# One graph and mixing block on one core: the mixing weights' product moved to the start, the value product ahead of the context sums, and 21 visits moved into the first graph layer

## The reference, cut to what matters

```python
xn = layernorm(x)
# mixing branch
q = softmax(xn @ Wq.T, axis=-1) * 512 ** -0.5
k = softmax(xn @ Wk.T, axis=-2)            # over the rows
v = xn @ Wv.T
context = k.T @ v                          # 512 x 512
y = q @ context + xn
mix = y @ W1.T @ W2.T + y
# graph branch, two layers
h = xn @ gW1.T + gb1
agg = segment_sum(h[src], dst)             # = A @ h, A counts the edges
z = relu(agg)                              # and again with gW2, gb2
x = x + graph + mix
# then a routed expert layer on layernorm(x), in the last third of the span
```

## Time and profile before

| | us |
|---|---|
| median of 3 runs | 469.31 (467.96 to 470.11) |
| the profiled execution's own time | 468.61 |
| span of its profile | 466.8 |
| TensorE busy | 451.0 of the span (97%) |
| VectorE busy | 320.9 (69%) |
| ScalarE / GpSimd busy | 150.6 / 63.1 |
| granted TensorE clock, mean | 1.00 in the profile's rows |

### The profile page before, as it was taken

How to read it: one execution, slowest core, us unless ns; L and a number is a source line. 1 busy time by engine, 2 the same in 40 slices (tenths; PEclk the granted TensorE clock), 3 DMA queues, 4 the chain that set the end, 5 groups by cost and what they waited for, 6 DMA issues and landing times.

```text
span 466.8 us, 6816 instructions
## 1 busy us (share of the span) xinstructions
PE 451.0 (97%) x2424; PEld 360.6 (77%) x2424; DVE 320.9 (69%) x1104; ACT 150.6 (32%) x272; POOL 63.1 (14%) x90
## 2 busy tenths in 40 slices
PE   7999999999999999999999999999999998878995
PEld 3788778888888888888779999877777776655783
DVE  6995699899998988897752110444645666777972
ACT  4686453322323332332222110222133114551110
POOL 4088200000000000000004000002300000006642
PEclk9999999999999999999999999999999999999999
DMA  8902002911000000001200000002744449305891
GB/s 219 287 1 91 1 0 91 219 50 65 2 1 1 1 1 1 1 2 20 108 0 4 1 1 1 1 0 53 277 139 134 134 142 380 131 1 190 289 356 71
DMA packets 20846, 40.46 MB, mean 87 GB/s; under 512 B 2953, under 2 KB 3283, under 8 KB 20805
## 3 DMA queue, kind: packets, MB, share of 16 engines
q1 hardware_dynamic: 18549, 32.55, 22.4%
q0 software_dynamic: 2256, 7.39, 4.5%
HBM read 30.10 MB, written 10.31 MB: 87 GB/s over the span
## 4 chain that ended last, share of the span: by engine, by line
PE 86%; DVE 8%; ACT 2%; issue 1%; DMA 1%; SPq 0%; POOLq 0%; DVEq 0%
PE ps L736 46%; PE ps L1031 9%; PE ps L957 9%; PE ps L848 5%; PE ps L723 5%; PE ps L1167 2%; ACT scrap_a L1424 1%; PE ps L1048 1%; PE ps L1137 1%; DMA X<-in_x 1%; PE ps L880 1%; PE ps L770 1%; PE ps L984 1%; PE ps L1008 1%; PE ps L1078 1%
## 5 line engine op out<-in xcount | busy, mean ns | idle before, releaser
L1713 DVE TENSOR_SCALAR RING_D<-places,PLACES 125x170 bf16<-125x170 f16 (+1 forms) x239 | 63.5, 266 | 0.0
L1714 DVE TENSOR_SCALAR RING_S<-iota,HOME 125x128 bf16<-125x128 f16 x239 | 60.4, 253 | 0.0
L957 PE MATMUL ps<-AT,H1H 125*128 125x416 f32 (+1 forms) x108 | 38.0, 352 | 0.0
L957 PE MATMUL ps<-AT,H1L 125*128 125x416 f32 (+1 forms) x108 | 38.0, 351 | 0.0
L1031 PE MATMUL ps<-H2H,AT 125*125 125x512 f32 x90 | 36.1, 402 | 0.0
L1031 PE MATMUL ps<-H2L,AT 125*125 125x512 f32 x90 | 35.5, 394 | 0.0
L1048 PE MATMUL ps<-WE0H 128*128 128x512 f32 x129 | 35.4, 408 | 0.0
L1781 DVE TENSOR_TENSOR ps<-ps,bias 125x512 f32<-125x512 f32 x20 | 14.0, 700 | 27.9 <-PE ps L736 27.9
L1860 DVE SCALAR_TENSOR_TENSOR ZL<-ps,ZH 128x416 fp32r<-128x416 f32 (+1 forms) x12 | 6.3, 585 | 38.7 <-ACT ZH L1369 38.7
L723 PEld LDWEIGHTS ps<-RING_D,RING_S 125*125 125x125 bf16 x239 | 25.7, 136 | 7.9
L605 POOL TENSOR_TENSOR G2L<-RAW_G,G2H 128x512 fp32r<-128x512 f32 x4 | 5.0, 1287 | 192.2 <-ACT G2H L1186 192.2
(11 more groups left out here) (410 smaller groups left out, 1171.7 us busy)
## 6 DMA issues: line engine op xcount, KB each, us to landing
RAW_E<-in_experts SPq DMA_DIRECT2D x8, 1024.0 KB, 9.9
RAW_AGAIN<-in_experts SPq DMA_DIRECT2D x3, 1024.0 KB
X<-in_x SPq DMA_DIRECT2D x1, 2240.0 KB
out_x<-X SPq DMA_DIRECT2D x10, 224.0 KB
scratch<-X SPq DMA_DIRECT2D x10, 224.0 KB
scratch<-Y SPq DMA_DIRECT2D x10, 224.0 KB
RAW_K<-in_WkT SPq DMA_DIRECT2D x4, 256.0 KB, 4.2
RAW<-in_mW2T SPq DMA_DIRECT2D x1, 1024.0 KB, 11.8
```

What stands on the lines that cost most here:

```text
L957: pe.matmul(place(f), h[0:TT, k, 128 * f:128 * (f + 1)], AT[0:TT, k, c0:c1], start=(k == 0 and n == 0), stop=False)
L1713: V.tensor_scalar(hot_d(v, width(b)), places[0:ET, 0:width(b)], PLACES[0:ET, c:c + 1], None, ALU.is_equal)
L1714: V.tensor_scalar(hot_s(v), iota[0:ET, :], HOME[0:ET, c:c + 1], None, ALU.is_equal).then_inc(done["marked"], 1)
```

## The change

What it does, engine by engine:

- **Loads.** W1 and W2 come first, by chunks (`load_pair`), mixed with x tiles 0 and 1; then Wk in four pieces, then the rest of x and the edges. The load of the gate's weights at the start goes, and `gsums` with it: the column sums are taken as one more column of `quads(0)` near the end.
- **mp** runs first on TensorE, with the chunk of the contraction as the outer loop and four open banks (2, 3, 6, 7). 9 warm-ups stand ahead of it, none behind. The turning of x tile 0 stands ahead of its fourth chunk, the identity matmuls in that chunk. ScalarE splits the pairs first and stores `mp` among its work of the K stage; VectorE makes all W1 rests and `mix_left`; GpSimd makes all four W2 rests first.
- **vp** takes the place that `mp` had, between K and context; it has no visits in it.
- **Context:** the last two tiles run with the column block outermost. The splits of Wq take the place of those of Wv.
- **cp** runs behind `ks`, with the contraction chunk outermost, in banks 6, 7, 0, 1, with 8 groups of 3 visits. VectorE marks 2 groups ahead of `total_left`, 6 behind `value_scale`, then makes the four `context_left`, then marks 4 groups.
- **h** has 5 visits in each tile (2 at its first matmul, 3 at its seventh) up to `h8`, where it had 3.

```diff
-WARM, WARMER = 12, 8
+WARM = 9
...
+MIX_BANKS, VALUE_BANKS = (2, 3, 6, 7), (6, 7, 0, 1)
...
-    spots = [("vp0", 6, 3)]
-    for u in ("vp1", "vp2", "vp3", "cp0", "cp1", "cp2", "cp3"):
-        spots += [(u, n, 3) for n in (0, 6)]
+    spots = [("cp", n, 3) for n in range(0, 48, 6)]
...
-    spots += [(f"h{i}", 6, 3) for i in range(NT)]
+    for i in range(NT - 1):
+        spots += [(f"h{i}", 0, 2), (f"h{i}", 6, 3)]
...
+            load_pair(0)
+            load_pair(1)
             load_x(0)
+            load_pair(2)
+            load_x(1)
+            load_pair(3)
             load_wk(0)
             load_wk(1)
-            load_x(1)
-            sp.dma_start(gw1[:], rows(gate_w[0])).then_inc(loads["gate1"], 16)
             load_wk(2)
             load_wk(3)
...
+            for c in range(C):
+                split_lo("w2", c)
             for v in sorted(set(VISITS)):
...
             warm(WARM)
-            pe.wait_ge(done["consts"], 1)
...
+            for c in range(C - 1):
+                pe.wait_ge(*hi_of("w2", c))
+                for f in range(C):
+                    mix_weights(c, f, 0, 0, first=(c == 0))
+                pe.wait_ge(*lo_of("w1", c))
+                for f in range(C):
+                    mix_weights(c, f, 1, 0)
+                pe.wait_ge(*lo_of("w2", c))
+                for f in range(C):
+                    mix_weights(c, f, 0, 1)
+            pe.wait_ge(done["consts"], 1)
             turn_x(0)
+            pe.wait_ge(*lo_of("w1", C - 1))
+            pe.wait_ge(*lo_of("w2", C - 1))
+            for f in range(C):
+                mix_weights(C - 1, f, 0, 0)
+                pe.matmul(PS[plan[f"mp{f}"][0]][:, 128 * f:128 * (f + 1)], ident[:], ident[:], start=False, stop=False)
+                mix_weights(C - 1, f, 1, 0)
+                closes(f"mp{f}", mix_weights(C - 1, f, 0, 1, last=True))
...
-                product(f"mp{c}", ps[:], (block_of(W1H, c), block_of(W1L, c)), (rows_of(W2H), rows_of(W2L)), before=add_one,
+                product(f"vp{c}", opens(f"vp{c}")[:], (block_of(WVH, c), block_of(WVL, c)), (rows_of(MPH), rows_of(MPL)),
                         between=peak_rows if c == 1 else None, at=8)
...
-            for c in range(C):
-                product(f"cp{c}", opens(f"cp{c}")[:], (block_of(TH, c), block_of(TL, c)), (rows_of(VPH), rows_of(VPL)),
-                        before=vp_ready if c == 0 else None, unit=f"cp{c}")
+            for c in range(C):
+                pe.wait_ge(done["tl_ready"], c + 1)
+                for f in range(C):
+                    ps = opens(f"cp{f}") if c == 0 else PS[plan[f"cp{f}"][0]]
+                    for k, (t, v) in enumerate(((TH, VPH), (TH, VPL), (TL, VPH))):
+                        visits("cp", n)
+                        n += 1
+                        mm = pe.matmul(ps[:], t[:, c, 128 * f:128 * (f + 1)], v[:, c, :], start=(c == 0 and k == 0),
+                                       stop=(c == C - 1 and k == 2))
+                    if c == C - 1:
+                        closes(f"cp{f}", mm)
...
+            for c in range(C // 2):
+                split_lo("w1", c)
             moments(0, statistics(0))
             normalise(0)
+            split_lo("w1", C - 2)
+            moments(1, statistics(1))
+            normalise(1)
+            split_lo("w1", C - 1)
             split_lo("wk", 0)
-            moments(1, statistics(1))
             x_left(0)
-            normalise(1)
...
-            for c in range(C):
-                value_left(c)
-                if c == 0:
-                    value_scale()
-                mark_next()
-                split_lo("wq", c)
-                mark_next()
+            for c in range(C):
+                total_left(c)
+            value_scale()
+            mark_next(6)
             for c in range(C):
                 context_left(c)
-                mark_next(2)
+            mark_next(4)
...
             for i in range(NT):
+                if marked[0] < len(CHUNKS_OF_VISITS):
+                    mark_next(2)
                 add_bias(1, i)
                 if i:
                     h1_left(i - 1)
-                if marked[0] < len(CHUNKS_OF_VISITS):
-                    mark_next()
```

More of the change, by code:

```diff
@@ L95, in turned @@
         if i < NT:
-            use(f"xt{i}", high, ("xth_ready", i + 1), ("xtl_ready", i + 1))
+            use(f"xt{i}", (4, 5) if i < 4 else high, ("xth_ready", i + 1), ("xtl_ready", i + 1))
+    for c, b in enumerate(MIX_BANKS):
+        use(f"mp{c}", (b,), ("mph_ready", c + 1), ("mpl_ready", c + 1))
     turned(0)
     turned(1)
-    use("gsums", (3,), ("gsum_ready", 1))
     for i in range(NT):
@@ L621, in _ @@
                 rest_of_x(i)
-            for c in range(C):
-                split_lo("w2", c)
-            split_lo("w1", 0)
-            split_lo("w1", 2)
+            split_lo("wv", 0)
+            split_lo("wv", 2)
             for i in range(4, NT):
                 rest_of_x(i)
-            reads(pool, f"mp{C - 1}")
+            reads(pool, f"k{NT - 1}")
+            pool.wait_ge(done["xnl_ready"], NT)
             link(nc.gpsimd.memset(first[:, 0:VISITS[0]], 0.0))
@@ L775, in wk_ready, with mix_weights @@
                 pe.wait_ge(*lo_of("wk", c))
-            turn_x(0)
-            pe.wait_ge(loads["gate1"], 16)
-            ps = opens("gsums")
-            for c in range(C):
-                mm = pe.matmul(ps[0:TT, 0:NE], ones[:, 0:TT], gw1[:, c, :], start=(c == 0), stop=(c == C - 1))
-            closes("gsums", mm)
-            warm(WARMER - 4)
+            def mix_weights(c, f, a, b, first=False, last=False):
+                w = ((W1H, W1L)[a], (W2H, W2L)[b])
+                return pe.matmul(PS[plan[f"mp{f}"][0]][:], w[0][:, c, 128 * f:128 * (f + 1)], w[1][:, c, :], start=first, stop=last)
+            for c in range(C - 1):
[9 more added lines that the diff above has]
+            pe.wait_ge(done["consts"], 1)
+            turn_x(0)
+            pe.wait_ge(*lo_of("w1", C - 1))
[5 more added lines that the diff above has]
+                closes(f"mp{f}", mix_weights(C - 1, f, 0, 1, last=True))
             for i in range(NT):
                 pe.wait_ge(done["xtl_ready"], i + 1)
-                inside = {0: (1, 4), 1: (2, 4), 2: (3, 5), 4: (5, 3)}.get(i)
+                inside = {0: (1, 4), 1: (2, 5), 2: (3, 5), 4: (5, 3)}.get(i)
                 kw = dict(between=lambda: turn_x(inside[0]), at=inside[1]) if inside else {}
@@ L1223, in store_k, with store_mix @@
                 copy(K[0:TT, i, :], ps_of(f"k{i}")[0:TT, :]).then_inc(done["k_stored"], 1)
-            root(0)
+            def store_mix(c):
+                reads(act, f"mp{c}")
+                copy(MPH[:, c, :], ps_of(f"mp{c}")[:]).then_inc(done["mph_ready"], 1)
+            for c in range(C):
+                split_hi("w1", c)
+                split_hi("w2", c)
+                if c in (1, 2):
+                    root(c - 1)
             split_hi("wk", 0)
@@ L1287, in _ @@
             for c in range(C):
-                reads(act, f"mp{c}")
-                copy(MPH[:, c, :], ps_of(f"mp{c}")[:]).then_inc(done["mph_ready"], 1)
+                reads(act, f"vp{c}")
+                copy(VPH[:, c, :], ps_of(f"vp{c}")[:]).then_inc(done["vph_ready"], 1)
                 exp_k(c)
@@ L1319, in store_counts @@
                 nc.scalar.activation(AT[0:TT, :, lo:hi], counts_of(g), ACT.Copy).then_inc(done["adj_hi"], 1)
-            for c in range(C):
-                groups_ending(f"vp{c}")
-                reads(act, f"vp{c}")
-                copy(VPH[:, c, :], ps_of(f"vp{c}")[:]).then_inc(done["vph_ready"], 1)
-                split_hi("wq", c)
+            groups_ending("cp", 0, 48)
             def round_q(i):
@@ L1544, in _ @@
             normalise(3)
+            mix_left(1)
             statistics(5)
+            x_left(3)
             peak(0)
-            x_left(3)
+            mix_left(2)
             statistics(6)
@@ L1551, in _ @@
             normalise(4)
+            mix_left(3)
             peak(1)
@@ L1662, in _ @@
             row_keys()
-            mix_left(3)
+            value_left(3)
             shift(3)
```

182 lines of the change are left out of this document (89 added, 93 removed).

## The result

The changed kernel takes **472.31 us** (median of 6 runs, 470.97 to 473.62); the kernel before, in the same session, 468.28 us (467.88 to 470.11). The ratio is 1.0084, with a 95% interval of 1.0067 to 1.0102: slower by 0.8%. The prediction was 470.6 us in a range of 466.0 to 474.3; the range held, the sign of the centre was right (+1.8 us forecast against the profiled execution of before, +3.3 measured between the two profiled executions, 471.93 against 468.61), and the outcome that came, slower by over 0.5%, had been given 0.36, less than "within 0.5%".

The account below looks back on a forecast made before the run. TensorE, busy 97% of the span, was taken to bound the kernel. Terms of +10.15 - 12.9 + 2.8 + 1.7 + 0.1 = +1.8 us put the profiled 468.6 at 470.4; 470.6 was given, range 466.0 to 474.3.

Parts of the forecast that it names:

- (4): Between K and context: `vp` goes from there, 48 matmuls and 7 groups of visits, -12.9 us.
- (5): Ahead of `q0`: its visits are marked only behind all four `context_left`, so TensorE waits, +2.8 us (bounds 0 and 3.3).
- quick rival: Fourth `mp` chunk does not wait, K not held up, wait ahead of `q0` short or absent: 465 to 468.5 us; chance 0.30.
- (1): The start: `mp` runs first, its fourth chunk waits for W1 3; K begins at 19.3 us instead of 9.35, +9.95.
- The end of 20.5: K's start at 20.5 us if each such VectorE operation between 6 and 16 us can lose a whole GpSimd instruction.
- (2): K stage: VectorE's 28.83 us grow by 2.4, TensorE waits 1.2 us against 0.8, +0.4 us (bounds -0.8 and +3).
- slow rival: VectorE sets the pace from 6 to 40 us, late x tiles make TensorE wait in K: 472.5 to 476 us; chance 0.17.
- (3): Between K and the end of context: only one identity matmul's saving counts, the rest becomes a longer wait, -0.2 us.
- (6): q stage: same groups at the same places, 4 groups of lead as before, 0 us.
- (7): `h` stage: 21 visits more cost TensorE +1.7 us; VectorE keeps up, 2.85 us against a tile of 3.2.
- rival 0.05: Visits bind in `h`: at 0.51 us per visit on VectorE a tile takes 3.75 us, +4.4, 475 us; chance 0.05.

Follow-up runs that it names:

- experiment 1: Kernel after with VectorE's marks around `q0` reordered, the first group ahead of `context_left(0)`; 468.61 us, ratio 1.0017 to the kernel before.
- experiment 5: Kernel after with one visit more in each of the last four tiles' third `x` group, so the last visits fall in `h7`; 470.86 us, one run.
- experiment 3: Kernel after with 3 and 3 visits instead of 2 and 3 in each `h` tile, so the last group is in `h7`; 472.45 us, one run.
- 4: Kernel after with GpSimd's fourth W2 rest held until VectorE's fourth W1 rest is done, TensorE waiting for it only at its first matmul; 472.26 us, one run.
- kernel 9: Kernel after with x tile 0's statistics and normalisation ahead of the second W1 rest and the second pair's halves; 474.32 us, one run.
- kernel 2: Kernel after with the last W1 and W2 pair handled ahead of x tile 1's root and normalisation; 470.51 us, ratio 1.0068 to the kernel before.

## Why the prediction was right, and where it was off

The mechanism held at each large step, and the terms of it were sized one by one:

- **(4) and (5), right.** -12.9 and +2.8 forecast, -12.9 and +2.9 measured. The wait at `q0` came from the order in which VectorE's list is written, and experiment 1 shows that by taking it away with another order. The quick rival (0.30) needed this wait short or absent and is out.
- **(1), 0.74 too small.** 19.3 forecast, 20.04 measured. The rest of W1 3 ended at 16.21 and not at 15.7. The step that failed is the landing of the second pair: I had taken the loads to keep ahead of TensorE at one per 0.8 to 1.05 us, and asked only what TensorE needs, while VectorE's list stood at the second W1 rest from 4.9 to 8.27 and began the statistics of tile 0 at 8.88 instead of 7.9. I had also counted the statistics of tile 1 twice (0.85, too much) and put 0.8 for the collisions where there was one of 1.09; two of them at my own 0.5 to 0.9 would have made 15.9 at least. So the value was nearly right by errors that cancel, which is luck. One reading under it was loose as well: the slow XF of the earlier trace rows, 9.71 to 10.99, did not end with GpSimd's subtraction, which ended at 10.71. The last chunk took 3.77 instead of 3.6. The end of 20.5, which I had set beside the Trainium skill's rule, was nearer than my own value, but for another reason: only one collision of this kind fell on VectorE's list, and the late landing did the rest.
- **(2), the sign was wrong, at 0.5 us.** +0.4 forecast, -0.16 measured. VectorE was busy 27.25 of 32.48 us, not 28.83 + 2.4, in 61 operations against 62: I had added what comes into the stage and left out what had moved ahead of it. TensorE waits once, 0.28 us, where I put 1.2. The slow rival (0.17), which lived on this, did not occur.
- **(3), 0.2 too favourable.** Its saving went into waits for `diag` (0.84 instead of 0.33) and EL (0.67 instead of 0.31).
- **(6), missed, +0.5.** I took the q stage as untouched, with 4 groups of lead. TensorE waits 0.3 us for QTL there; the other 0.2 I did not find.
- **(7), the price of a visit right, the end of the stage missed.** +1.87 for 21 visits against +1.7 (the terms as I had them add up to 1.8). The claim that `h` would have no idle TensorE was wrong: the counts of the last three visits, now in `h8`, are stored at 249.81, and the aggregation pays 0.32 us of gap; experiment 5 takes it away. Marks did not bind at five a tile (rival 0.05 out), and at six they cost 0.5 us (experiment 3).
- **The step that was not there at all: the clock.** An idle TensorE was priced at its length. In about half of the executions with the wait at `q0` (9 of 15) the wait costs up to 1.6 us more through the clock. The profiled execution is one without the fall.

In sum, the terms missed by 1.5 us, which makes +3.4 in the profiles of the forecast +1.8: the start 0.7, K and the context stage -0.35, `q0`, q, `h` and the end 1.2. That alone is over 0.5%, the 2.35 us up to which I had called it the same. The medians differ by +4.0 (472.31 less 468.28). Of the 0.7 us that this is above the profiled executions' +3.3, 0.4 is the median of the kernel after above its profiled execution, where the clock's fall has its part; 0.3 is the profiled execution of the kernel before above its own median, and no effect of the change.

What stays open: why the second pair lands anywhere from 6.35 to 7.78 us, what the last 0.2 us of the q stage is, and the three low-clock executions of the kernel before, none of which was profiled. That the landing sets K's start rests on the fixed distance in five profiles, on the chain and on VectorE's list without idle time, not on an experiment that moved it.

## What to carry to other kernels

When a product is moved to fill an idle start, follow the list of the vector engine from the first load that it waits for, not only TensorE's, and at each place where an engine's results come in one burst (banks that all close together): work that others wait for is to be ahead of the burst, with the ring wide enough to hold it. A wait of TensorE of 2 us may cost more than its length through the clock (up to 1.6 us more here, in about half of the executions); give it something to do or take it away. The full clock came at 5.1 to 7.6 us here, at another time in each execution, so price the first matmuls behind the warm-ups at the lower clock. Then price the last user of a moved piece (here the counts of the last visits), since it is that which the next stage waits for.

## What the runs showed of the hardware that was not expected

- A wait of TensorE of 2 us, with four visits (170 columns each) behind it, goes, in 9 of 15 executions by the mean clock and in the profiles of kernels 3, 4, 5 and 9, with a fall of the granted clock from 1.00 to 0.50 for 3.4 us. It begins 0.6, 2.2 and 0.7 us after work has resumed in kernels 3, 4 and 5, and 0.1 us before it in kernel 9. With eight matmuls of no use in the wait none of 6 executions has it.
- The first group of four `mp` matmuls took 1.27 us in the kernel after and 2.20 in kernel 2, and anything between in the others. It is the clock: behind warm-ups that begin at 2.17 us in every profile, the distance of the starts drops from 0.42 us to 0.22 or 0.23 at 5.06 us at the earliest (kernel after) and 7.55 at the latest (kernel 2), each time where the trace's first entry of the granted clock stands. Ahead of that entry a window reads 1.00 although the matmuls run at half of that.
- Two subtractions of 128 x 512 that take 0.68 us on VectorE and 1.29 on GpSimd take 1.77 and 1.34 when GpSimd's begins first, 0.68 and 1.66 when VectorE's does.
- The second pair of W1 and W2 (256 KB each), asked for at 1.72 and 2.18 us behind the first pair and ahead of tile 0 of x, was used only at 6.35 to 7.78 us in nine profiles, and its scatter goes into K's start.
